# A second pass of attention that takes its scores and its value matmuls two groups at a time

## The reference

```python
qh = (q @ Wq.T + bq).reshape(B, Sq, 16, 16)
kh = (k @ Wk.T + bk).reshape(B, Sk, 16, 16)       # Sk = 12544
vh = (v @ Wv.T + bv).reshape(B, Sk, 16, 16)
scores = jnp.einsum('bqhd,bkhd->bhqk', qh, kh) / np.sqrt(16)
scores = jnp.where(attention_mask[:, None, :, :], NEG_FILL, scores)
out = jnp.einsum('bhqk,bkhd->bqhd', jax.nn.softmax(scores, axis=-1), vh)
```

## Time and profile before

| | us |
|---|---|
| median of 3 runs (563.46 to 565.96) | 564.08 |
| the profiled execution | 566.53 |
| its span, first to last instruction | 564.9 |
| of it the second pass, first scores to last value matmul | 283.5 to 503.4 |
| TensorE busy | 520.6 (92%) |
| ScalarE busy | 386.1 (68%) |
| exponentials of the second pass (112) | 186.5 |

### The profile page before, as it was taken

One profiled execution on the slowest core, in us unless ns is written; L12 is line 12 of the kernel. 1 busy time (PEld: TensorE's weight loads), 2 busy tenths in 40 slices (PEclk: granted clock), 3 DMA queues, 4 the chain that ended last, 5 costly groups with the idle time before them and its releaser, 6 DMA issues.

```text
span 564.9 us, 14212 instructions
## 1 busy us (share of the span) xinstructions
PE 520.6 (92%) x5620; PEld 435.1 (77%) x5620; DVE 300.0 (53%) x432; ACT 386.1 (68%) x377; POOL 101.7 (18%) x101
## 2 busy tenths in 40 slices
PE   5799989999999999999389999999999999979997
PEld 3699978898888988898278888887887888866543
DVE  5758978898888988899849500000000000007565
ACT  3258767777777677776268888888888888852211
POOL 5583322233312333112200000000000000000000
PEclk9889999999999999999769999999999999999799
DMA  8564567655676556994943667777766676500000
GB/s 283 162 255 132 204 228 280 216 181 201 242 280 231 180 188 242 331 361 180 361 194 113 251 251 251 275 280 279 259 238 245 236 263 236 194 3 1 1 0 9
DMA packets 34758, 117.45 MB, mean 208 GB/s; under 512 B 4400, under 2 KB 10416, under 8 KB 34736
## 3 DMA queue, kind: packets, MB, share of 16 engines
q1 hardware_dynamic: 30560, 110.58, 53.6%
q0 software_dynamic: 4032, 6.42, 4.4%
q10 hardware_dynamic: 144, 0.13, 0.1%
HBM read 74.44 MB, written 39.47 MB: 202 GB/s over the span
## 4 chain that ended last, share of the span: by engine, by line
PE 50%; DMA 17%; issue 9%; DVE 8%; POOL 8%; ACT 4%; SPq 2%; POOLq 0%; ACTq 0%; DVEq 0%
PE ps_a L944 17%; PE ps_k L958 15%; DMA early<-in_ctx 12%; POOL k_stack L339 8%; DMA k_stack<-k_hi_scratch 4%; PE ps_k L810 4%; PE ps_a L852 4%; PE ps_a L819 3%; ACT k_stack L395 3%; SPq L277 2%; PE ps_a L861 1%; DMA v_in<-in_wv 1%; PE ps_a L887 1%; PE ps_a L1088 1%; DVE early L654 1%
## 5 line engine op out<-in xcount | busy, mean ns | idle before, releaser
L626 DVE TENSOR_REDUCE block_max<-ps_a 128x1 f32<-128x896 f32 x112 | 121.6, 1086 | 11.4 <-PE ps_a L852 8.9
L944 PE MATMUL ps_a<-q_stack,k_stack 128*128 128x256 f32 x784 | 124.8, 300 | 2.9 <-DMA k_stack<-k_hi_scratch 1.4
L944 PEld LDWEIGHTS ps_a<-q_stack,k_stack 128*128 128x128 f32 x784 | 101.7, 192 | 27.1 <-issue 21.8
L852 PE MATMUL ps_a<-k_hi,q_pad 128*128 128x448 f32 x448 | 110.4, 368 | 2.6 <-DVE block_max L626 2.6
L431 ACT CAST early<-ps_a 128x896 bf16<-128x896 f32 x104 | 94.3, 906 | 23.6 <-PE ps_a L852 23.5
L484 ACT ACTIVATE middle<-ps_a 128x2048 f32<-128x2048 f32 (+1 forms) x56 | 93.2, 1666 | 18.3 <-PE ps_a L944 17.7
L484 ACT ACTIVATE early<-ps_a 128x2048 f32<-128x2048 f32 (+1 forms) x56 | 93.3, 1666 | 15.2 <-PE ps_a L944 14.6
L687 DVE COPY early<-ps_k 128x512 f32<-128x512 f32 x1 | 0.7, 691 | 188.1 <-PE ps_a L997 188.1
L852 PEld LDWEIGHTS ps_a<-k_hi,q_pad 128*128 128x128 f32 x448 | 79.7, 189 | 10.6 <-DVE block_max L626 4.1
L339 POOL TENSOR_TENSOR k_stack<-early,k_stack 128x448 fp32r<-128x448 f32 x52 | 59.6, 1150 | 147.2 <-DVE early L621 120.5
L810 PE MATMUL ps_k<-k_stack,w_hi 128*128 128x448 f32 x224 | 59.0, 386 | 14.5 <-DVE k_lo L579 9.5
(11 more groups left out here) (174 smaller groups left out, 455.7 us busy)
## 6 DMA issues: line engine op xcount, KB each, us to landing
k_stack<-k_hi_scratch SPq DMA_DIRECT2D x56, 448.0 KB, 6.1
v_scratch<-early SPq DMA_DIRECT2D x14, 952.0 KB, 8.1
v_in<-v_scratch SPq DMA_DIRECT2D x14, 952.0 KB, 8.9
early<-in_ctx SPq DMA_DIRECT2D x14, 896.0 KB, 6.7
k_hi_scratch<-k_hi SPq DMA_DIRECT2D x28, 448.0 KB, 7.0
k_lo_scratch<-k_lo SPq DMA_DIRECT2D x28, 448.0 KB, 6.9
k_stack<-k_lo_scratch SPq DMA_DIRECT2D x28, 448.0 KB, 6.0
mask_b<-in_maskn POOLq DMA_DIRECT2D x14, 224.0 KB, 6.8
```

Source lines behind the costliest of these rows:

```text
L626: nc.vector.tensor_reduce(block_max[:, par, taken:taken + 1], ps_a[:, 2 * BUFFER[par][h]:2 * BUFFER[par][h] + 2, 0:HK], AX.XY, ALU.max).th ...
L852: last = nc.tensor.matmul(out, q_pad[:, h, :], k_hi[:, par, m, n * HK:(n + 1) * HK], start=True, stop=not masked)
L944: last = nc.tensor.matmul(ps_a[:, bank, (k % 2) * 2 * Q:(k % 2 + 1) * 2 * Q], k_stack[:, b_par, a, t * P:(t + 1) * P], q_stack[:, a, :, :] ...
```

## The change

In `two_blocks` the loop goes over the groups in twos. For u and u + 1 it first waits for each one's exponential and does the scores of the group two on, one after the other, and then does the value matmuls of both groups. The sizes of the groups change places: 6 pairs first, in banks 0 to 2, then 8 in banks 3 to 6. In the last step, where no scores are left, both waits for the exponentials stand ahead of the values. On SP the key loads of block b now wait until all scores up to block b - 2 are done (`scored`); the value load still waits for the value matmuls, and has its wait behind the key loads.

```diff
-UP = (8, 6)
+UP = (6, 8)
...
                 for par in range(2):
                     b = i * 2 + par
+                    sp.wait_ge(scored, (b - 1) * UNITS)
+                    load_keys(b, par)
                     sp.wait_ge(prob_slots_free, (b - 1) * UNITS + SLOTS_P)
-                    load_keys(b, par)
                     load_values(b, par)
...
-                    for u in range(2 * UNITS):
-                        n = i * (2 * UNITS) + u
-                        pe.wait_ge(exp_done, n + 1)
-                        if not (final and u >= 2 * UNITS - 2):
-                            nxt = (u + 2) % (2 * UNITS)
-                            if nxt == 0:
-                                arrive(i * 2 + 2, 0)
-                            if nxt == UNITS:
-                                pe.wait_ge(consts_set, 8)
-                                arrive(i * 2 + 1, 1)
-                            score(nxt // UNITS, nxt % UNITS)
+                    for u in range(0, 2 * UNITS, 2):
+                        for w in (u, u + 1):
+                            pe.wait_ge(exp_done, i * (2 * UNITS) + w + 1)
+                            if not (final and u == 2 * UNITS - 2):
+                                nxt = (w + 2) % (2 * UNITS)
+                                if nxt == 0:
+                                    arrive(i * 2 + 2, 0)
+                                if nxt == UNITS:
+                                    pe.wait_ge(consts_set, 8)
+                                    arrive(i * 2 + 1, 1)
+                                score(nxt // UNITS, nxt % UNITS)
                         if u % UNITS == 0:
                             pe.wait_ge(v_back[u // UNITS], i * 16 + 16)
-                        add_up(u // UNITS, u % UNITS, u % SLOTS_P)
+                        for w in (u, u + 1):
+                            add_up(w // UNITS, w % UNITS, w % SLOTS_P)
```

## The result

| | before | after |
|---|---|---|
| median of the runs, us | 564.54 (563.46 to 565.96, 4 runs) | 549.65 (549.36 to 550.72, 4 runs) |
| the profiled execution | 566.53 | 549.37 |
| its span | 564.9 | 547.7 |
| second pass, first scores to last value matmul | 283.50 to 503.37 | 282.40 to 484.28 |
| from the scores of the third pair of groups to those of the 56th | 204.72 | 187.82 |

The ratio of after to before is 0.9747, with a 95% interval of 0.9711 to 0.9783: 14.9 us by the medians, where 13.4 were forecast (550.7).

The account below looks back on a forecast made before the run. TensorE's own sequence was taken to set the second pass's period. Steady periods -12.5, key waits -1.5, start 0 and end +0.6 sum to -13.4 us, so 564.08 becomes 550.7; range 545 to 558.5.

Parts of the forecast that it names:

- TensorE's own sequence sets the period: Second pass before the change: TensorE's sequence, not waits for ScalarE, gives the 3.835 us period.
- The gaps: TensorE, per period: values behind values save 0.15 us, scores behind scores 0.15; TensorE alone then needs 3.55.
- The wait for the second exponential: Ahead of both value groups: a loop over two periods through ScalarE takes 7.20 us, 3.60 a period.
- Saved per period 0.235: Steady part of the second pass: 0.235 us less a period, 12.5 us over 53 periods.
- The key loads: SP's earlier key loads: slack about 3.6 us, so the key waits go; gain 1.5 us, bounds 0 and 1.5.
- Start and end: Second pass: start changes by zero, bounds +1.0 and -0.5; end takes 6.1 us in place of 5.51, +0.6.
- B: Rival, chance 0.12: the gap ahead of scores comes with the semaphore wait, not the tile; period 3.78, 560.3 us.
- C: Rival, chance 0.08: TensorE gains more than the rows say and ScalarE runs back to back; 538.6 us.
- D: Rival, chance 0.07: DMA gives the block's time, which stays at 4 x 3.835; 564 us.
- E: Rival, chance 0.06: TensorE's clock drops with a short wait every period; ten periods at 1.2 GHz give 580 us.
- the signs named: Trace if right: periods 3.55 to 3.65 us, two weight-load gaps, ScalarE idle 0.2 ahead of 1536 form, no key waits.

Follow-up runs that it names:

- the zeros: Changed kernel plus one whole-array matmul of zeros a period: between the two value groups 564.60 us, ahead of both 551.57 us.

## Why the prediction was right

The sign and the size (550.7 against 549.65) came out of the mechanism that was named. That the time is right to 1 us is partly luck: the second pass gained 2.9 us more than the sum had, and the medians 1.2 us less than the traces' terms add up to. Step by step:

- *TensorE's own sequence sets the period; the two gaps ahead of scores are no waits for ScalarE.* Right. Three satisfied waits cost nothing, and one matmul that brings back two changes of tile costs the gain.
- *The gaps.* Values behind values: 1.44 and 0.21, right to the hundredth. Scores behind scores: 14 up to the values take 412.73 - 410.87 = 1.86 where nothing waits, against 1.90. TensorE alone needs 1.86 + 1.65 = 3.51 us, not 3.55: the 0.125 a score was 0.12.
- *The wait for the second exponential, a loop over two periods.* Right, and this decides the period. Measured at 410.87: 1.02 to the short exponential, 3.22 for both, 0.06 to the second group's scores (415.11 to 415.17), 2.80 to the scores at 417.97. That is 7.10, forecast 7.20. The term that was mis-sized is ScalarE's pair, 3.35 in the forecast and 3.22 in fact. I had read in the earlier trace rows that the short exponential follows the long one with 0.02 between and took that for back to back. It was not: its scores began at 407.22 and were ready 1.01 later, at 408.23 (the changed kernel has 1.02 from scores to the short exponential), just where it started. Back to back, ScalarE overlaps two instructions by 0.1 us, which the trace of before did not have at any place in the steady part (3.35 to 3.37 for each pair). It did have it at the start of the pass, in a row that the prediction used for something else: 3.22 for the first two. Had I read both, the loop would have come out at 7.07, 3.54 a period. The rows' "0.6 idle" of the short form hid a wait that ended within hundredths of the other engine. The alternation (3.51, 3.59) is the mark of this loop: a period in which the second scores waited makes the next one start late enough for them not to wait. The short exponential of before, which the reading rests on:

```profile
408.23 1.45 ACT L484 ACTIVATE early<-ps_a 128x1536 f32<-128x1536 f32 x1
```

- *Saved per period 0.235, 12.5 us, and 1.5 for the keys.* The sum 14.0 measured 16.9; 0.29 a period instead of 0.235.
- *The key loads.* The waits went, as said. What the prediction did not say is that with late keys the pairs would have made the waits longer; it priced that part by the waits of before, 1.5 us, and beside the pairs it is worth 4 to 7.
- *Start and end.* The end is right: 6.1 us, forecast 6.1, against 5.5. The start is longer by 0.1 to 0.5 us where the clock comes back early (7.94 to 8.40 against 7.87), and by 0.2 to 0.5 where it comes late (9.80 to 10.09 against 9.64); zero was forecast, with +1.0 and -0.5 as bounds.
- *Rivals.* B (waits) fell by the added waits, and by the changed kernel's own wait between the two groups of scores, which leaves no gap. C (ScalarE back to back) did not come: 0.3 us idle a period. D: no wait for data, with 4 periods at 14.2 us a block. E: the granted clock is 1.00 from 305 to 484 us.
- *Slips of reading.* The granted clock is 9 or more tenths from slice 22 of the earlier trace rows on, not from 21, which has a 6 and is where the pass starts. It rose at 291.6 us, not 291. The range's lower end, 545, is nearly half of the way to rival C and not a third. None of them changes the forecast. Of the signs named, the period fell just under its bounds (3.544 against 3.55 to 3.65) and ScalarE's idle is 0.3 instead of 0.2.

By the traces' terms, with some 0.2 us for the start, the medians should differ by 16.9 - 0.2 - 0.6 = 16.1 us; they differ by 14.9, and the interval (12.2 to 16.3) holds both that and the forecast. The runs can't settle more.

## What to carry to other kernels

Where TensorE alternates between matmuls of two tile shapes, group them: here, at a granted clock of 1.00, two changes of tile cost some 0.2 us and the head of each group of scores another 0.07 (the latter is worked out, not tried), whatever the waits are. The order that groups them puts the consumer's wait ahead of more work; write down the loop through the other engine, and count over how many periods it runs, since a stall that comes every other period costs half. And a buffer that is refilled on the slower of two releases has to be looked at again whenever the period gets shorter: a load that was just in time is late then.

## What the runs showed of the hardware

- A whole-array weight load behind value matmuls (128*17 tiles) starts 0.21 us after the last of their loads ends; behind whole-array matmuls there is no gap, or 0.05 us (ahead of the zeros). Two changes of tile cost 0.22 us together (periods of 3.799 and 3.579 us). A wait on a semaphore already reached costs nothing that these traces show on TensorE, even inside a group of loads: 56 value records in 1.44 us, with and without.
- ScalarE starts the next instruction about 0.1 us before the one ahead ends when its data are there (1.45 + 1.87 in 3.22), so an instruction that takes 0.25 alone costs 0.14 in a row.
- After TensorE's idle of 8.4 us between the passes, the clock came back 3.2 us behind the first scores in one execution and 8.1 behind them in another with the same work on TensorE up to there. By the third pair of groups that makes 1.8 us (7.87 against 9.64), more than some of the parts that were tested.
